# Eight-head layer of a graph network: TensorE gathers eight of a chunk's 64 edge steps by one-hot products

## The reference, cut to what matters

```python
h = (x @ W).reshape(n, heads, out_ch)                       # 8 heads x 8 channels
a_src = jnp.einsum('nhc,hc->nh', h, att_src)
a_dst = jnp.einsum('nhc,hc->nh', h, att_dst)
logits = jax.nn.leaky_relu(a_src[src] + a_dst[dst], NEG_SLOPE)
m = jax.ops.segment_max(logits, dst, num_segments=n)
e = jnp.exp(logits - m[dst])
denom = jax.ops.segment_sum(e, dst, num_segments=n)
msgs = h[src] * (e / denom[dst])[:, :, None]
out = jax.ops.segment_sum(msgs, dst, num_segments=n)
```

## Time and profile before

| | us |
|---|---|
| median of three runs | 3327.02 |
| the profiled execution's own time | 3327.11 |
| its span on the core | 3325.3 |
| span with PE busy | 2793.2 |
| span with DVE busy | 1770.5 |
| span with ACT busy | 1383.9 |
| span with POOL busy | 970.5 |

### The profile page before, as it was taken

The page is one execution under the profiler, slowest core; times in us unless marked ns, Lnnn a source line. Parts: engine busy times, 40 slices in busy tenths (PEclk is TensorE's granted clock), DMA queues, the critical chain, the costliest instruction groups (busy, mean ns, idle before and its releaser), DMA issues. The chain is left out here.

```text
span 3325.3 us, 42240 instructions
## 1 busy us (share of the span) xinstructions
PE 2793.2 (84%) x14474; PEld 2097.3 (63%) x14474; DVE 1770.5 (53%) x4020; ACT 1383.9 (42%) x2629; POOL 970.5 (29%) x785
## 2 busy tenths in 40 slices
PE   5778887999996999999999999999864444456997
PEld 3445774777775877878877787785423333344775
DVE  8998657999967541121122121112664444447994
ACT  4573235999995221121111111111333333333896
POOL 6110070000001632213322222230277777750000
PEclk9999897999998999999999999999756666666999
DMA  5334442111002522212211213110211111113200
GB/s 161 137 112 151 180 163 89 41 55 70 1 1 95 197 102 86 76 58 89 94 60 70 88 65 125 60 65 7 74 31 29 29 29 29 29 20 129 80 36 20
DMA packets 73828, 252.16 MB, mean 76 GB/s; under 512 B 20459, under 2 KB 52784, under 8 KB 63920
## 3 DMA queue, kind: packets, MB, share of 16 engines
q1 hardware_dynamic: 56728, 222.19, 17.7%
q0 software_dynamic: 16896, 27.27, 3.8%
HBM read 218.24 MB, written 31.17 MB: 75 GB/s over the span
## 5 line engine op out<-in xcount | busy, mean ns | idle before, releaser
L2961 PE MATMUL psum<-gate_stream,parts 128*128 128x384 f32 (+1 forms) x3600 | 668.9, 344 | 8.6 <-ACT x L3001 4.4
L2961 PEld LDWEIGHTS psum<-gate_stream,parts 128*128 128x128 f32 x3600 | 631.6, 189 | 25.5 <-issue 6.1
L3066 POOL CAST gate_stream<-gate_adj 128x1920 fp32r<-128x1920 f16 (+1 forms) x200 | 372.2, 1868 | 836.2 <-PE psum L2961 826.4
L2321 PE MATMUL psum<-gat_h,gat_pair 128*128 128x129 f32 (+1 forms) x3750 | 571.1, 292 | 10.4 <-DVE gat_pair L2125 9.5
L2321 PEld LDWEIGHTS psum<-gat_h,gat_pair 128*128 128x128 f32 (+1 forms) x3750 | 460.9, 190 | 126.2 <-issue 77.7
L1637 POOL DMA_INDIRECT edge_rows<-edge_table,src_idx x440 | 436.4, 992 | 184.8 <-issue 133.5
L3099 DVE SCALAR_TENSOR_TENSOR gate_work<-psum,bhh,gate_work 128x384 f32<-128x384 f32 (+1 forms) x80 | 50.1, 626 | 780.8 <-PE psum L2908 763.1
L2125 DVE SCALAR_TENSOR_TENSOR gat_pair<-gat_above,gat_adj 128x512 f32<-128x512 f32 (+3 forms) x525 | 328.7, 626 | 87.4 <-PE psum L2321 58.0
L2234 ACT ACTIVATE gat_above<-psum,gat_as 128x512 f32<-128x512 f32 (+3 forms) x525 | 329.4, 627 | 42.9 <-PE psum L2309 41.2
L2225 ACT ACTIVATE psum<-gat_ad_rows,gat_as 128x512 f32<-128x512 f32 (+3 forms) x525 | 334.9, 638 | 16.9
L2080 DVE SCALAR_TENSOR_TENSOR gat_acc<-gat_adj,gat_q,gat_acc 128x512 f32<-128x512 f16 (+3 forms) x497 | 330.7, 683 | 0.0
(11 more groups left out here) (497 smaller groups left out, 3918.9 us busy)
## 6 DMA issues: line engine op xcount, KB each, us to landing
gate_adj<-adj SPq DMA_DIRECT2D x35, 2400.0 KB, 8.1
gat_adj<-adj SPq DMA_DIRECT2D x8, 3200.0 KB, 11.0
gcn_adj<-adj SPq DMA_DIRECT2D x10, 2400.0 KB, 8.5
adj<-count_stage SPq DMA_DIRECT2D x196, 100.0 KB, 1.7
gate_adj<-adj SPq DMA_DIRECT2D x5, 2800.0 KB, 9.0
edge_rows<-edge_table,src_idx POOLq DMA_INDIRECT x440, 2.5
gcn_adj<-adj SPq DMA_DIRECT2D x2, 3200.0 KB, 10.2
gcn_adj<-adj SPq DMA_DIRECT2D x2, 2800.0 KB, 10.0
```

Source lines behind the costliest of these rows:

```text
L2321: mm = e.matmul(ps[0:p, b, a:a + D + 1], pair[:, g % 2, i * P:i * P + p], h1[:, hi, h, :], start=hi == 0 and i % 3 == 0, stop=hi == NT - 1 ...
L2961: mm = e.matmul(ps[:, f, 0:hi - lo], parts[:, t, m, f, :], stream[:, (NGG * i + t // GG) % GR, 0:windows(i), t % GG * W:(t % GG + 1) * W], ...
L3066: e.tensor_copy(stream[:, n % GR, 0:windows(i), :], cols[:, i % 2, 0:windows(i), g * GW:(g + 1) * GW]).then_inc(widened, 1)
```

## The change

POOL gathers fewer steps: of the chunks' steps the last 4, 8, 8, 8, 8, 8, 0 and 0 (`DRAWN`) come in another way, in batches of four steps (`EG`): 44 steps, 11 batches. For a batch, PE spreads the source numbers of its 512 edges over the partitions (`sources`), ACT copies them to an f16 tile (`lay`), DVE compares them with the numbers of the 128 nodes of each of 25 node tiles (`find`, 25 comparisons of 128x512 into a ring of 12), and PE multiplies each result with that tile's rows (`pull`: for each tile four matmuls of 216 columns, bf16, since the f32 rows are split in three bf16 parts). The 25 tiles add up in PSUM banks 6 and 7, and DVE adds the three parts into `rows` (`draw`, two reductions).

Where it is put: the one batch of chunk 0 stands ahead of the first look-up, behind the splitting of the rows (`near`, three copies on ACT and two subtractions on DVE). For chunks 1 to 5, the first batch runs inside the chain of scans of the chunk before, in four shares of 8, 4, 4 and 9 tiles; the second runs in the sums of the chunk before, one tile after each second step, in the place of that step's `keep_busy`. The source numbers of the chunk after next are laid out between the sums and the look-ups.

Besides: the ends and carries of the chain move from PSUM bank 7 to bank 4, so `ends_of(c)` waits for `taken` of chunk c - 1; `clear` comes behind `peaks_of`; each `widen` gets a `keep_busy` ahead of it; chunk 7 shares a buffer with chunk 6 and its gathers wait for nothing; several working tiles move to tiles that are free, and semaphores are merged. The source numbers are written as f16 (`sf`, one more DVE instruction of 64x896 and one more DMA), and read back as `src_rows` (one more DMA beside `place_rows`).

```diff
 CHUNKS = (64, 64, 64, 64, 64, 64, 32, 24)
+DRAWN = (4, 8, 8, 8, 8, 8, 0, 0)
+NSRC = NP // 2 - 32
+RING = 12
...
     def sync_places(self, e):
         e.wait_ge(self.made, 11)
         e.dma_start(self.k.row_scratch.rearrange("(j p q) -> p j q", j=KJ, p=KP), self.bf[:]).then_inc(self.kept, 16)
+        e.dma_start(self.k.src_scratch.rearrange("(j p q) -> p j q", j=KJ, p=KP), self.sf[:]).then_inc(self.kept, 16)
...
+        e.tensor_scalar(self.sf[:], part(0), -float(NSRC), None, ALU.add)
         e.tensor_tensor(self.bf[:], part(1), self.win128[:].unsqueeze(2).to_broadcast([KP, KJ, P]), ALU.subtract).then_inc(made, 1)
...
-        small = ps[:, 7, 0:P]
+        small = ps[:, 4, SUMS + 3:SUMS + 3 + P]
         ends = small.rearrange("p (w s) -> p w s", w=2)
         back = small.rearrange("p (n s) -> p n s", s=SROWS)
         product = ps[:, 5, 0:EG * 3 * HEADS]
         size, first_step = CHUNKS, CHUNK_AT
+        by_pool = [size[c] - DRAWN[c] for c in range(end + 1)]
+        batches = [(c, s) for c in range(end + 1) for s in range(by_pool[c], size[c], EG)]
...
+        def in_chain(c):
+
+            at = of_chunk[c + 1]
+            return ([(at[0], 0, 8)], [(at[0], 8, 12)], [(at[0], 12, 16)], [(at[0], 16, NT)]) if len(at) == 2 else ([],) * 4
+
+        def in_sums(c):
+
+            return of_chunk[c + 1][-1:]
...
-                    if c >= 2:
+                    if 2 <= c < end:
                         e.wait_ge(summed, c - 1)
-                    for s in range(size[c]):
+                    for s in range(by_pool[c]):
                         k = first_step[c] + s
-                        e.indirect_dma_start(out=rows[:, c % 2, s, 0:ROWS], out_offset=None, in_=table,
+                        e.indirect_dma_start(out=row(c)[:, s, 0:ROWS], out_offset=None, in_=table,
                                              in_offset=bass.IndirectOffsetOnAxis(ap=self.src_idx[:, k:k + 1], axis=0)
-                                             ).then_inc(fetched[c % 2], 16)
+                                             ).then_inc(fetched[arrival[c]], 16)
...
+                def find(share):
+
+                    for m, lo, hi in share:
+                        if lo == 0:
+                            e.wait_ge(src_in, m + 1)
+                        for t in range(lo, hi):
+                            n = m * NT + t
+                            if n >= RING:
+                                e.wait_ge(pulled, n - RING + 1)
+                            e.tensor_scalar(one[:, n % RING, :], src_wide[:, m % 2, :], self.tile_ids[:, t:t + 1], None,
+                                            ALU.is_equal).then_inc(ones, 1)
+
+                def draw(m):
+
+                    c, s = batches[m]
+                    e.wait_ge(pulled, (m + 1) * NT)
+                    if 2 <= c:
+                        e.wait_ge(summed, min(c - 1, end - 2))
+                    for j in range(2):
+                        of = ps[:, 6 + j, 0:6 * ROWS].rearrange("p (s n w) -> p s w n", n=3, w=ROWS)
+                        inst = e.tensor_reduce(row(c)[:, s + 2 * j:s + 2 * j + 2, 0:ROWS], of, AX.X, ALU.add)
+                    inst.then_inc(drawn, 1)
...
+                e.wait_ge(split, 1)
+                e.tensor_tensor(part[:, :, 0:ROWS], acc[:], parts[:, :, 0, :], ALU.subtract).then_inc(begun, 1)
...
+                e.wait_ge(split, 2)
+                e.tensor_tensor(part[:, :, 0:ROWS], part[:, :, 0:ROWS], parts[:, :, 1, :], ALU.subtract).then_inc(begun, 1)
...
+                for m in of_chunk[0]:
+                    find([(m, 0, NT)])
+                    draw(m)
...
                     e.scalar_tensor_tensor(logit[:, 0:n], logit[:, 0:n], NEG, logit[:, 0:n], ALU.mult, ALU.max).then_inc(logits, 1)
+                    find(share[0])
...
+                    find(share[1])
                     if 0 < c < end:
                         join_most(c - 1)
...
+                    find(share[2])
...
+                    e.tensor_reduce(carried[:], chosen[:], AX.X, ALU.add).then_inc(carried_in, 1)
+                    find(share[3])
...
+                    e.tensor_tensor(fwd[:, 0:whole], fwd[:, 0:whole], bwd[:, 0:whole], ALU.max).then_inc(second, 1)
+                    if share[0]:
+                        draw(of_chunk[c + 1][0])
                     if 0 < c < end:
                         join_sums(c - 1)
...
-                                    ALU.mult).then_inc(scaled, 1)
+                    e.tensor_tensor(by_head(row(c)[:, :, 0:64]), by_head(row(c)[:, :, 0:64]), channels(weight[:, 0:n]),
+                                    ALU.mult).then_inc(marks, 1)
+                    for m in in_sums(c):
+                        find([(m, 0, NT)])
+                        draw(m)
                 for c in (end - 1, end):
...
+                def lay(c):
+
+                    for m in of_chunk[c]:
+                        e.wait_ge(src_up, m + 1)
+                        if m >= 2:
+                            e.wait_ge(ones, (m - 1) * NT)
+                        e.copy(src_wide[:, m % 2, :], ps[:, 6 + m % 2, :]).then_inc(src_in, 1)
+
+                def near(n):
+
+                    if n:
+                        e.wait_ge(begun, 2 * n - 1)
+                    e.copy(parts[:, :, n, :], part[:, :, 0:ROWS] if n else acc[:]).then_inc(split, 1)
+
+                near(0)
+                lay(0)
+                near(1)
+                near(2)
...
                     if 0 < c < end:
+                        lay(c + 1)
                         take(c - 1)
...
+                    if c == 0:
+                        lay(1)
...
+                def broadcast(bank, g, table_rows):
+
+                    return e.matmul(ps[:, bank, :], ident_b[:, g:g + 1].to_broadcast([groups, P]), table_rows[:], start=True, stop=True)
+
                 def widen(g):
 
                     if g >= 2:
                         e.wait_ge(hots_t, g - 1)
-                    e.matmul(ps[:, 6 + g % 2, :], ident_b[:, g:g + 1].to_broadcast([groups, P]), self.place_rows[:],
-                             start=True, stop=True).then_inc(wide, 1)
+                    self.keep_busy(e, ps[:, 6 + g % 2, :], 1)
+                    broadcast(6 + g % 2, g, self.place_rows).then_inc(wide, 1)
...
+                def sources(c):
+
+                    for m in of_chunk[c]:
+                        if of_chunk[c][0]:
+                            e.wait_ge(drawn, of_chunk[c][0])
+                        broadcast(6 + m % 2, (first_step[c] + batches[m][1]) // EG, self.src_rows).then_inc(src_up, 1)
+
+                def pull(share):
+
+                    for m, lo, hi in share:
+                        if lo == 0:
+                            e.wait_ge(src_in, of_chunk[batches[m][0]][-1] + 1)
+                            if m:
+                                e.wait_ge(drawn, m)
+                            for b in (6, 7):
+                                e.matmul(ps[:, b, 0:6 * ROWS], zero[:, 0:P], zero[:, 0:6 * ROWS], start=True, stop=False,
+                                         skip_group_check=True)
+                        for t in range(lo, hi):
+                            e.wait_ge(ones, m * NT + t + 1)
+                            for s in range(EG):
+                                mm = e.matmul(ps[:, 6 + s // 2, (s % 2) * 3 * ROWS:(s % 2 + 1) * 3 * ROWS],
+                                              one[:, (m * NT + t) % RING, s * P:(s + 1) * P],
+                                              parts[:, t].rearrange("p n w -> p (n w)"), start=False, stop=t == NT - 1,
+                                              skip_group_check=True)
...
+                    e.wait_ge(first, 2 * c + 2)
+                    if c:
+                        e.wait_ge(taken, c)
+                    else:
+                        e.wait_ge(copied, 2)
...
+                    every = 2 if size[c] == KP else 1
...
+                        pulls = [(m, (s - 4) // every, (s - 4) // every + 1) for m in in_sums(c)
+                                 if s >= 4 and (s - 4) % every == 0 and (s - 4) // every < NT]
+                        pull(pulls)
+                        if not pulls and s < size[c] - 1:
+                            self.keep_busy(e, ps[:, 5, :], 1)
+                    for m in in_sums(c):
+                        pull([(m, -(-(size[c] - 4) // every), NT)])
...
+                e.wait_ge(copied, 1)
+                sources(0)
+                e.wait_ge(split, 3)
+                for m in of_chunk[0]:
+                    pull([(m, 0, NT)])
+                e.wait_ge(drawn, len(of_chunk[0]))
+                e.wait_ge(begun, 7)
+                for c in range(end + 1):
+                    share = in_chain(c)
+                    look_ups(c)
+                    if c == 0:
+                        e.wait_ge(hots_t, due[0])
+                        sources(1)
                     line_up(c)
-                    if c == 0:
-                        e.wait_ge(copied, 2)
```

(51 more changed lines are left out.)

127 lines of the change are left out of this document (63 added, 64 removed).

## The result

The changed kernel takes 3350.52 us (median of 4 runs, 3349.19 to 3355.27) where the kernel before, run beside it, takes 3324.28 us (4 runs, 3319.02 to 3329.48): a ratio of 1.0081, with an interval of 1.0068 to 1.0094. It is slower by 26.2 us. The forecast was +40, with a range that holds the time: the sign and the mechanism were right, and three terms of the sum were too large. The profiled execution has a span of 3349.0 us against 3325.3, 23.7 us more. Not all of such a difference belongs to the change. Inside the stage, from DVE's first instruction to the start of that copy, the change costs 21.6 us (604.4 us before, 626.1 after).

What follows compares the result with a forecast made beforehand. Gathers bound the kernel, at 83.4 us a period. Start +22.3, chain +38.5, sums +45.0, between chunks +8.4, DMA waits -74.0 give +40.2 us on 3327.1: 3367 us, range 3335 to 3400.

Steps and rivals of the forecast that it cites:

- three terms of the sum: Chunks 0 to 4: work added in the chain +38.5 us, in the sums +45.0, between chunks +8.4.
- The first, that the comparisons stall POOL: Rival: DVE's comparisons stretch POOL's gathers twofold through chain and sums, gathers bind again; about 3430 us; chance 0.06.
- The third, a dearer chain: Rival: PE at half clock is last in the chain, +13.9 us instead of 7.7; 3398 us; chance 0.13.
- The second: Rival: PE keeps full clock up to the sums, tiles take 0.36 us, batches fit; 3329 us; chance 0.14.
- the cheap tile alone: Tile of 0.36 us in the pulls with the clock unchanged: about +20 us, counted in the forecast's own case.
- 68.5 us of other work: Per period, look-ups, chain, weighting and sums of the other engines in one line, beside gathers setting 83.4 us.
- DMA waits of 74.0 us: DVE's five waits for gathers before `masked` of chunks 1 to 5; all would go, -74.0 us.
- The start: Ahead of the first look-up: splitting the rows and chunk 0's batch add 21.7 us, 22.3 with `src_rows` and `sf`.
- The tile of `pull`: Four PE matmuls of 216 columns, columns plus 22 ns each: 0.45 us at full clock, 0.82 at half.
- The chain: Scans of chunks 0 to 4: `find` 6.75 less 0.9, `draw` 1.2, PE 0.6; 7.7 us a chunk, 38.5 for five.
- The 0.6 us for a PE that lags: In the chain: PE at half clock some 2 us behind DVE after the first share, mostly covered; 0.6 us a chunk.
- Between chunks: Four times, two spreads on PE and ACT's two copies ahead of the look-ups: 2.1 us each, 8.4 in all.

Runs made afterwards that it cites:

- the one-part run: Changed kernel with pulls multiplying only one of the three bf16 parts, 72 columns instead of 216; 3325.21 us, ratio 0.9996.

## Why the prediction was right, and where it missed

*The rivals.* The first, that the comparisons stall POOL, is refuted by the 0.94 and 0.95 us gathers and by the 56 gathers of a chunk, which take 74.7 us where 56 x 1.25 + 3.5 is 73.5. By the rule of the Trainium skill (SBUF — State Buffer, "two separate sides") DVE work in a 2-port mode locks GpSimd out, and so does work with two SBUF inputs against GpSimd work that reads SBUF. Here the f32 additions of two tiles do stretch gathers (1.43 to 2.32 us), and the f16 comparisons of one SBUF tile against a per-partition value hardly do (0.961 us); no trace shows in which mode these ran. The third, a dearer chain, is refuted by the one-part run. The second had two halves: the cheap tiles came true, the full clock did not (the sums start at 0.50 and the look-ups never leave it), and half of it, the cheap tile alone, is nearly the case that was measured. It was put at "about +20 us", but the prediction's own terms give more: with 0.36 us for 0.45 and 0.72 for 0.82 the five sums are some 11 us shorter and the start 2, which leaves about +27, and +26 was measured. That half should have been the forecast.

*The bound and its change.* Right: 68.5 us of other work, DMA waits of 74.0 us that all go, POOL waiting for the sums instead. Its waits were put at some 14 us and are 8.8 to 10.9: the period is 84 us and not 87, and the gathers take 1.2 us more.

*The start.* 21.7 us forecast, 19.2 measured for split and batch. The pulls were put at 14.1 us and take 11.3. Some 1.8 us of that are the error in the tile (0.37 us for 0.45, at half clock 0.72 for 0.82), and 1.0 that the clock rises 4.0 us behind the first pull, where 6.2 were carried over from the sums. The 3.6 us later start of the stage, which varies by itself, fills the gap: that this line came out at +22.6 is luck.

*The tile of `pull`* is the step that failed most. 22 ns over the columns was carried from a row of matmuls of other shapes and types, which gave 0.45 us; it is 0.37, 92.5 ns for 216 columns, with each matmul on its own weights. The Trainium skill (TensorE: Matmul & The Clock Gate, "Back-to-back issue gap") gives N / 2.4 + 2.5 ns for a matmul by itself, which for 216 columns is 92.5 ns, and the trace agrees with that figure. For streams of weight load and matmul, which this is, it gives about 81 ns at 128 columns and 131 ns at 512 instead; an estimate on the line between these two is 92.5 ns as well, so 216 columns can't tell the two rules apart. In 25 tiles that is 2.0 us of the 9.0 us a chunk. The sums measured +7.3 a chunk, so the tile is about the whole of the miss, 8.4 us over five chunks.

*The chain.* 7.7 us forecast, 7.1 measured in a full chunk and 5.0 in chunk 0. The comparisons (0.28 for 0.27) and `draw` (1.1 for 1.2) were right, and 7.0 + 1.1 - 0.9 = 7.2. The 0.6 us for a PE that lags is the term that does not exist: the clock is 1.00 for the last share of the pulls, and PE ends 2.5 us before DVE asks. That chunk 0 pays only 5.0 was not foreseen, though the trace of the kernel before shows it. In chunk 0 there is no join of a chunk before, and DVE waits for PE three times in the chain: 0.77 us, the 0.88 of `carries_of`, and 1.21 us:

```profile
2487.07 0.28 DVE L1744 TENSOR_TENSOR_SCAN edge_carry<-rows_start,psum 8x64 f32<-8x64 f32 x1 [0.77 <-PE psum L1870]
...
2494.06 0.69 DVE L1770 TENSOR_TENSOR edge_top<-psum,edge_on_dst 128x512 f32<-128x512 f32 x1 [1.21 <-PE psum L1893]
```

`find` and `draw` fill these 2.9 us, none of the three waits is left in the changed kernel, and 7.0 + 1.1 - 2.9 = 5.2.

*Between chunks.* There are five, not four, up to `masked` of chunk 5: 1.6 to 1.9 us in each of four and 0.3 in the last, where 4 x 2.1 were forecast. `keep_busy`, the later `clear` and the moved waits cost nothing, as said: the run without any batch and the run without `keep_busy` show it.

*What was missed in the reasoning.* Nothing in the forecast asked for the best amount. With the two lines written down as they were, steps drawn = n gives (64 - n) x 1.25 + 3.5 against 68.5 + 9 n / 4: they cross near n = 4, at 78.5 against 77.5. The two runs with four steps a chunk sit there, 3304 us, 0.6% under the kernel before. No other amount was run. The formula also leaves out the 6.0 us of the split, which is paid once. A second batch takes 5 us off a line that is no longer last, and adds 7 to 9 to the one that is.

## What to carry to other kernels

Where an engine waits for another, write down both lines in the period, price the work that moves from one to the other, and move only as much as makes them equal; here half of the move (without the first batch) gains 19 us and the whole of it loses 26. Whether the work lands in the chain of one engine or among the work of another made little difference here (7.1 us against 6.7), since both lie in one serial line. Count also what the move costs once, here the 6 us of the split. For a repeated matmul take the price from its columns and a row of back-to-back matmuls of the same type, not from an average over others, and give a stage's start, which drifts from one execution to the next, no cause in the change.

## What the hardware showed

Comparisons of f16 against a per-partition value, 128 x 512 and back to back, left gathers issued by POOL at 0.94 to 1.04 us (mean of 80: 0.961); f32 additions of two tiles stretched them to 1.43 to 2.32 us, and 38 gathers beside comparisons and another operation took up to 1.65 us. Matmuls of 216 columns with a new weight load each follow each other in 92.5 ns at 2.4 GHz, 2.5 ns over their columns, and in 180 ns at 1.2 GHz, so the load is hidden; after matmuls of 72 columns the next f32 step takes 0.26 instead of 0.20 us. PE at 85% busy in the look-ups (42.26 of 50 us) stayed at a granted clock of 0.50 as at 72% without `keep_busy`.
